# A two-layer decoder on one core: another layout of the attention rounds in both layers

## What is computed

```python
x = x + _L0_attn_ref(_layernorm(x), ...)            # gated delta-rule scan
x = x + _L0_xattn_ref(_layernorm(x), ctx, ctx, ...) # 16 heads of 16, causal
x = x + _L0_ffn_ref(_layernorm(x), ...)             # 8 experts by low-rank parts, 1024 wide
x = x + _L1_attn_ref(_layernorm(x), ...)            # state-space scan, 512 inner, projected by out_proj
x = x + _L1_xattn_ref(_layernorm(x), ctx, ctx, ...) # 16 heads of 16, not causal
x = x + _L1_ffn_ref(_layernorm(x), ...)             # product keys
```

```python
scores = jnp.einsum('bthd,bshd->bhts', Q, K) / jnp.sqrt(jnp.float32(DH))
P = jax.nn.softmax(scores, axis=-1)
out = jnp.einsum('bhts,bshd->bthd', P, V).reshape(B, Tq, D)
return out @ Wo + b_o
```

## Time and profile before

| | us |
|---|---|
| median of 3 runs | 8376.84 (8373.83 to 8382.36) |
| the profiled execution: its own time | 8381.71 |
| the profiled execution: its span | 8379.6 |
| layer 0 stage, one turn (12 turns, 1607.86 to 2242.06) | 52.85 |
| layer 1 stage, one turn (14 turns, 6071.05 to 6764.23) | 49.51 |

### The profile page before, as it was taken

One profiled execution on the slowest core, in us unless ns is written; L12 is line 12 of the kernel. 1 busy time (PEld: TensorE's weight loads), 2 busy tenths in 40 slices (PEclk: granted clock), 3 DMA queues, 4 the chain that ended last, 5 costly groups with the idle time before them and its releaser, 6 DMA issues. The chain is left out here.

```text
span 8379.6 us, 122772 instructions
## 1 busy us (share of the span) xinstructions
PE 6244.1 (75%) x40740; PEld 4178.7 (50%) x40740; DVE 6666.1 (80%) x11381; ACT 3461.7 (41%) x6666; POOL 3671.7 (44%) x1911
## 2 busy tenths in 40 slices
PE   5455554888866677777777777777677769999999
PEld 3355554677755322222222222222244448888888
DVE  6799997555567899999999999999744547676765
ACT  3333332333323566666666566666444321212121
POOL 0000000111100599999999999999611112222222
PEclk8777776999988899999999999999888879999999
DMA  2211112111022100000000000000011110000000
GB/s 63 72 42 42 42 44 61 39 36 36 19 78 108 63 14 15 15 14 15 15 14 21 19 17 14 15 15 8 29 41 36 36 66 7 8 7 8 7 8 6
DMA packets 335677, 254.47 MB, mean 30 GB/s; under 512 B 161763, under 2 KB 307046, under 8 KB 334854
## 3 DMA queue, kind: packets, MB, share of 16 engines
q1 hardware_dynamic: 332774, 248.29, 9.5%
q10 hardware_dynamic: 2464, 0.26, 0.0%
HBM read 140.46 MB, written 108.00 MB: 30 GB/s over the span
## 5 line engine op out<-in xcount | busy, mean ns | idle before, releaser
L1809 POOL TENSOR_TENSOR ss_inp<-ss_dx,ss_b_all 128x1024 f32<-128x1024 f32 x1024 | 2390.2, 2359 | 230.1 <-ACT ss_b_all L1783 227.9
L1827 DVE TENSOR_TENSOR_SCAN ss_h<-banks,ss_inp 128x1024 f32<-128x1024 f32 x1024 | 2313.0, 2278 | 59.9 <-ACT banks L1775 59.9
L1747 PE MATMUL banks<-ss_ch,ident 128*128 128x512 f32 x4096 | 1959.5, 601 | 64.9 <-DVE ss_xc L1843 64.9
L1775 ACT ACTIVATE banks<-ss_dt,ss_neg_a 128x510 f32<-128x510 f32 x2048 | 1334.7, 688 | 2.7 <-DVE ss_h L1827 2.7
L1725 PE MATMUL banks<-ss_bc,ss_pick 96*128 96x512 bf16 x2048 | 747.0, 386 | 787.8 <-DVE ss_ch L1836 750.2
L1783 ACT COPY ss_b_all<-banks 128x512 f32<-128x512 f32 x1024 | 600.4, 586 | 1235.7 <-PE banks L1725 1232.0
L1747 PEld LDWEIGHTS banks<-ss_ch,ident 128*128 128x128 f32 x4096 | 788.0, 193 | 635.9 <-issue 577.9
L1725 PEld LDWEIGHTS banks<-ss_bc,ss_pick 96*128 (+1 forms) x2048 | 200.0, 98 | 1662.7 <-issue 1484.6
L1836 DVE TENSOR_TENSOR ss_ch<-ss_h,banks 128x1024 f32<-128x1024 f32 x768 | 917.9, 1195 | 0.0
L605 PE MATMUL banks<-ms_rprod,ident 128*128 128x128 f32 x2048 | 466.8, 400 | 507.9 <-DVE ms_rprod L691 507.9
L2139 POOL TENSOR_TENSOR pk_blockhot<-pk_onehot,pk_parts 128x2048 bf16<-128x2048 bf16 x96 | 345.5, 3628 | 1099.7 <-DVE pk_parts L2377 1099.7
(11 more groups left out here) (293 smaller groups left out, 10344.9 us busy)
## 6 DMA issues: line engine op xcount, KB each, us to landing
keep_v<-ms_cx_values SPq DMA_DIRECT2D x32, 512.0 KB, 2.8
l_va<-keep_v SPq DMA_DIRECT2D x32, 512.0 KB, 5.3
l_kf<-keep_k SPq DMA_DIRECT2D x32, 256.0 KB, 4.1
keep_x<-l_x SPq DMA_DIRECT2D x32, 256.0 KB, 2.2
keep_xc<-si_xc SPq DMA_DIRECT2D x16, 512.0 KB, 3.0
keep_zs<-si_zs SPq DMA_DIRECT2D x16, 512.0 KB, 4.0
keep_dt<-si_acc SPq DMA_DIRECT2D x16, 512.0 KB, 2.6
keep_dx<-si_acc SPq DMA_DIRECT2D x16, 512.0 KB, 2.6
```

The lines of the kernel that those rows point to most:

```text
L1747: m = T_.matmul(sums[j][:, :], chip.ident[:, :], ch[u][:, j, :], start=first, stop=False, skip_group_check=True)
L1775: last = A.activation(decay[u % 2][:, j, :, 1:T], inputs[i % 2][0][:, j, :, 1:T], ACT.Exp, scale=neg_a[:, i % 2 * HB + j, bass.ds(k * UN + ...
L1809: G_.tensor_tensor(inp[u][:, :, :], inputs[i % 2][1][:, :, :, :].rearrange("p j g t -> p j (g t)"), rep(b_all[u][:, :], 1, HB), ALU.mult). ...
L1827: V.tensor_tensor_scan(flat(h[u][:, :, :]), decay[u % 2].rearrange("p j g t -> p (j g t)"), flat(inp[u][:, :, :]), 0.0, ALU.mult, ALU.add) ...
```

## The change

In both layers the scores (and their maxima) begin a round later: score s of a batch stood in round 2 + s and stands in round 3 + s of its turns, one round behind the one in which it stood; `forward_*` of layer 0 starts one round later too. `enter_vector` and `enter_scalar` are cut in two: the part up to the biased q, and `parts_*`, the split of q. Layer 0 puts them together as before, with a wait for `q_split` of the batch ahead added before the bias.

In layer 1 a turn is laid out anew. Heads start in round 7 (scores so in rounds 10 to 25), the norm and q projection of batch n + 2 in rounds 0 to 8, the split of q moves to the next turn (batch n + 1, DVE rounds 1 to 6), and the projection of the scan's output is taken out of `enter` as `mix_*`, for batch n + 3, in four quarters in rounds 19 to 22. The outer loop starts one turn earlier, and SP loads four batches ahead instead of three.

```diff
     def maxima_tensor(self, T_, b):
-        yield
-        yield
+        yield from nothing(3)
...
-    def enter_tensor(T_, b):
-        yield
+    def mix_tensor(T_, b):
         T_.wait_ge(*ys_loaded[b % 2].at(b // 2))
         if b:
             T_.wait_ge(*at.q_biased.at(b - 1))
         for t in range(NT):
-            m = project(T_, bank[at.ENTER], tiled(ys[b % 2], t), blocks(wout), col=t * C)
-            if t == NT - 1:
-                m.then_inc(ys_projected.sem, 1)
-            yield
-        yield from nothing(8)
-        yield from at.enter_tensor(T_, b)
-
-    def enter_vector(V, b):
+            for half in range(2):
+                for j in range(half * IB // 2, (half + 1) * IB // 2):
+                    m = T_.matmul(bank[at.ENTER][:, t * C:(t + 1) * C], ys[b % 2][:, j, t * P:(t + 1) * P], wout[:, j, :],
+                                  start=j == 0, stop=j == IB - 1)
+                if t == NT - 1 and half:
+                    m.then_inc(ys_projected.sem, 1)
+                yield
...
+    TURNS, MIX = 7, 19
+
     def tensor(T_):
-        for n in range(-2, B):
+        for n in range(-3, B):
             now = []
             if n >= 0:
                 now.append(at.weigh_tensor(T_, n))
             if 0 <= n + 1 < B:
-                now.append(at.maxima_tensor(T_, n + 1))
-            if n + 2 < B:
-                now.append(enter_tensor(T_, n + 2))
+                now.append(after(TURNS, at.maxima_tensor(T_, n + 1)))
+            if 0 <= n + 2 < B:
+                now.append(after(4, at.enter_tensor(T_, n + 2)))
+            if n + 3 < B:
+                now.append(after(MIX, mix_tensor(T_, n + 3)))
             if 0 <= n + 1 < B:
-                now.append(at.turns_tensor(T_, n + 1))
+                now.append(after(TURNS, at.turns_tensor(T_, n + 1)))
             rounds(now)
...
             if 0 <= n < B:
                 now.append(at.weigh_vector(V, n, x_ready))
+            if 0 <= n + 2 < B:
+                now.append(enter_vector(V, n + 2))
             if 0 <= n + 1 < B:
-                now.append(at.maxima_vector(V, n + 1))
+                now.append(after(1, at.parts_vector(V, n + 1)))
+                now.append(after(TURNS, at.maxima_vector(V, n + 1)))
             if n >= 1:
                 now.append(after(2, measure(V, n - 1)))
-            if n + 2 < B:
-                now.append(enter_vector(V, n + 2))
+            if n + 3 < B:
+                now.append(after(MIX + 4, mix_vector(V, n + 3)))
             if 0 <= n + 1 < B:
-                now.append(at.turns_vector(V, n + 1))
+                now.append(after(TURNS, at.turns_vector(V, n + 1)))
```

More of the change, by code:

```diff
@@ L896, in enter_vector, with parts_vector @@
         V.wait_ge(*self.q_projected.at(b))
+        if b:
+            V.wait_ge(*self.q_split.at(b - 1))
         V.tensor_tensor(self.qf[:, :, :], two(self.bank[self.ENTER][:, :]), rep(self.bq[:, :], 1, NT), ALU.add).then_inc(self.q_biased.sem, 1)
         yield
-        yield from nothing(2)
+    def parts_vector(self, V, b):
         V.wait_ge(*self.q_biased.at(b))
@@ L922, in enter_scalar, with parts_scalar @@
         yield
-        yield from nothing(11)
+    def parts_scalar(self, A, b):
         A.wait_ge(*self.q_split.at(b))
@@ L1270, in enter_vector, with enter_scalar @@
         yield from at.enter_vector(V, b)
+        yield from nothing(2)
+        yield from at.parts_vector(V, b)
+    def enter_scalar(A, b):
+        yield from nothing(11)
+        yield from at.enter_scalar(A, b)
+        yield from nothing(11)
+        yield from at.parts_scalar(A, b)
     def forward_tensor(T_, b):
@@ L1351, in tensor @@
             if n >= 1:
-                now.append(forward_tensor(T_, n - 1))
+                now.append(after(1, forward_tensor(T_, n - 1)))
             if 0 <= n + 1 < B:
@@ L1366, in vector @@
             if n >= 1:
-                now.append(forward_vector(V, n - 1))
+                now.append(after(1, forward_vector(V, n - 1)))
             if n + 2 < B:
@@ L1379, in scalar @@
             if n + 2 < B:
-                now.append(after(11, at.enter_scalar(A, n + 2)))
+                now.append(enter_scalar(A, n + 2))
             if 0 <= n + 1 < B:
@@ L1946, in sync @@
         load(0)
-        for n in range(-2, B):
-            if n + 3 < B:
-                load(n + 3)
+        for n in range(-3, B):
+            if n + 4 < B:
+                load(n + 4)
             if 0 <= n + 1 < B:
@@ L1964, in enter_tensor, with mix_vector @@
         for t in range(NT):
-            m = project(T_, bank[at.ENTER], tiled(ys[b % 2], t), blocks(wout), col=t * C)
-            if t == NT - 1:
-                m.then_inc(ys_projected.sem, 1)
-            yield
-        yield from nothing(8)
-        yield from at.enter_tensor(T_, b)
-    def enter_vector(V, b):
+            for half in range(2):
[5 more added lines that the diff above has]
+                yield
+    def mix_vector(V, b):
         x = at.x[b % 5]
-        yield from nothing(4)
         V.wait_ge(*at.x_loaded[b % 5].at(b // 5))
@@ L1977, in enter_vector @@
         V.tensor_tensor(x[:, :, :], x[:, :, :], two(bank[at.ENTER][:, :]), ALU.add).then_inc(mixed.sem, 1)
-        yield from nothing(3)
+        yield
+    def enter_vector(V, b):
         V.wait_ge(*mixed.at(b))
@@ L1994, in tensor @@
             if 0 <= n + 1 < B:
[L1995 to L1997 removed]
+                now.append(after(TURNS, at.maxima_tensor(T_, n + 1)))
[3 more added lines that the diff above has]
+                now.append(after(MIX, mix_tensor(T_, n + 3)))
             if 0 <= n + 1 < B:
[L1999 removed]
+                now.append(after(TURNS, at.turns_tensor(T_, n + 1)))
             rounds(now)
     def vector(V):
[L2003 removed]
+        for n in range(-3, B + 1):
             now = []
@@ L2022, in scalar @@
             if n + 2 < B:
-                now.append(after(11, at.enter_scalar(A, n + 2)))
+                now.append(after(4, at.enter_scalar(A, n + 2)))
             if 0 <= n + 1 < B:
-                now.append(at.turns_scalar(A, n + 1))
+                now.append(after(TURNS - 1, at.parts_scalar(A, n + 1)))
+                now.append(after(TURNS, at.turns_scalar(A, n + 1)))
             rounds(now)
```

1 line of the change is left out of this document (removed).

## The result

The changed kernel takes 8257.42 us (median of 4 runs, 8255.1 to 8261.42), the kernel before 8376.57 in the same comparison (4 runs, 8373.83 to 8382.36). The ratio is 0.9857, with a 95% interval of 0.9844 to 0.9869: 119 us less. The forecast was 8281 (96 us less), its range 8225 to 8345.

The account below looks back on a forecast made before the run. PE was taken to bound layer 0, no engine layer 1, whose tail is one chain. Layer 1's 70 us less and layer 0's 26 less gave -96: 8286 against the profiled execution, 8281 against the median; range 8225 to 8345.

Parts of the forecast that it names:

- Rounds 0 to 6: Layer 1's turn start, left to rescoring, then norm transpose, values and q projection: 9.7 us, bounds 8.5 and 12.
- Rounds 7 to 18: Layer 1's full rounds: twelve at 1.55 make 18.6, less waits for qT, 17.5 us; bounds 14.5 and 20.
- Rounds 19 to 26: Layer 1's tail, from ot's copy to the norm's transpose, with scores, heads and mix over it: 17.3 us, bounds 15.5 and 20.
- Contention: Layer 1's tail: POOL's k split, sharing SBUF interfaces with DVE, makes the bias add 0.55 us longer.
- The cover of POOL: Layer 1's tail: norm2's root, queued behind POOL's split, done at 14.8, under reductions until 15.6: 0.8 us to spare.
- three waits: Layer 0, PE: nmaxT behind output adds 1.0 us, round 5's kT copy 1.7, division behind feed-forward cut and q subtraction 0.9.
- The ends: Layer 1's stage: +2 us before the first turn, where first heads come later; -2 in turn 14, with less tail.
- The clock was not lost in the body: Rival, 5 in 100: PE at 1.2 GHz through layer 1's rounds 7 to 22, +10 us a turn, 8421.
- The rounds did not keep their price: Rival, 6 in 100: hand-overs rule layer 1's rounds 7 to 25 at 1.91 us each, turn 49.0, total 8344.
- Layer 0 did not lose: Rival, 12 in 100: layer 0's new waits stand and old ones stay, +1.4 us in fifteen turns, total 8328.
- A late POOL: Layer 1: POOL or va's load late by 2 us a turn, 8309; within the forecast's range, no separate chance.
- The rule on the clock: Layer 1 before the change, clock 0.86 over 49.5 us: prices 6.9 us a turn, 97 in fourteen; not taken as gain.

Follow-up runs that it names:

- the other two edits: On the changed kernel: 36 spare matmuls in layer 1's tail, layer 0's output adds behind nmaxT; 8272.97 us with heads from round 4, 8283.7 from round 3.

## Why the prediction was right

**The bound and the mechanism held.** No engine bounded layer 1; the tail's chain did, and laying scores and heads over it shortened the turn. The wo projection at 1.95, the granted clock at 0.91, the h2 transpose waiting for DVE came as forecast. In size the forecast was cautious: 119 us came where 96 were forecast, 96 and 22 by layer (by the run with layer 1 alone) where it had 70 and 26. Three terms of layer 1's sum, 44.5 us, were too large; the usual turn took 41.78:

- *Rounds 0 to 6*: 9.7 forecast, 8.83 measured. The norm was ready sooner: the transpose of h1 stands 4.54 us behind that of the maxima, not 5.2, and the clock was back in the middle of the rescoring.
- *Rounds 7 to 18*: 17.5 forecast, 16.28 measured. "Twelve make 18.6" counted twelve full rounds. The scores only begin in round 10 and the rescoring ends in round 16, so three rounds lack a pair of scores (0.22 us each) and two lack rescoring (0.43 each): 1.5 us, more than the miss. The count in the window shows it: 155 matmuls, where twelve full rounds with their three weighings of values would hold 168.
- *Rounds 19 to 26*: 17.3 forecast, 16.67 measured, with errors inside. PE reached the wo projection at 6.16 (forecast 6.45), and the last reduction ended at 14.94 (forecast 15.6). Contention was too small: the bias add took 1.41 us, 0.73 more than in a tail with POOL idle, forecast 0.55. The pair of rows behind that price had 0.70 us of a POOL instruction still ahead of the subtraction, here it was 0.87. The cover of POOL was forecast at 0.8 us and there was none. The norm starts 0.11 us behind the end of POOL's root, as in the kernel before, where it had nothing else to wait for (0.10), and with less work on POOL it came 0.13 sooner. So the root ended last by 0.13 us. The prediction had named that as a sign of being wrong. Here it cost next to nothing; with the heads three rounds later it was 6.26 us, so the thin margin at round 7 was luck and not the planned cover.

**Layer 0**: three waits were forecast at 1.0, 1.7 and 0.9 us and came at 0.96, 1.20 and 0.90, their sum with the rest at 4.1 against 4.20. The turn lost 1.44 us where the listed waits fell by 1.62. That the two are so near is luck in part: "work is unchanged, so I sum PE's waits" is the weak step, since short delays aren't listed, and with the feed-forward early the listed waits fell by 1.05 while the turn grew by 0.69. The attribution was wrong as well. I put the removed waits of scores for qT first; the run with the feed-forward early shows that the scores' distance alone costs 0.69 us, and that the delayed feed-forward on top of it brings 2.13, all of the gain and more. The fourth corner, scores early with the feed-forward late, was not run, so whether the distance helps beside the delayed feed-forward stays open.

**The ends**: +4.4 before the first turn (forecast +2), -1.0 in turn 14 (forecast -2). The load of `va`, costed at nothing, cost 1.67 us in the first turn and nothing in the others.

**The rivals.** The clock was not lost in the body (1.00 in rounds 7 to 18). The rounds did not keep their price. Layer 0 did not lose. A late POOL cost 0.13 us at round 7; at round 10 DVE waits 6.26 us a turn for it, most of what the change had won.

**The rule on the clock** (the Trainium skill, TensorE: Matmul & The Clock Gate, Terms) puts the penalty at the throttled time times (1 - K/N). Worked with the mean granted clock, that is an estimate of 42.04 x (1 - 0.91) = 3.8 us a turn for the changed kernel, and of 3.4 for a rise from 0.91 to 0.99. The measured gain is 0.66 in the usual turn and 0.64 on the mean of fourteen, (588.51 - 579.62)/14. So the trace goes against reading that figure as a gain: here the low clock costs only where PE is the one that is waited for, at the two transposes that end a turn and at the first rescorings.

## What to carry to other kernels

Count what each round of a hand-made order really holds before multiplying a round's price: rounds at either end of a pipeline lack a member. When a chain is covered with other work, the cover queues in the chain's own engines, here as reductions on DVE and as the split on POOL. Look for the second line before shortening the first: less on DVE alone brought the tail nothing, less on POOL alone 0.13 us, and a head start in round 5, which shortens both, 1.48. (Of head starts in rounds 3, 4, 5, 7 and 10 the best is 5, 3 and 4 having been run only with the other two edits. q's parts stand against an earlier one, DVE's reductions and POOL's split against a later one.) And an order can be summed from listed waits only down to the shortest wait that is listed: undo each half by itself before saying which half brought the gain.

## What the runs showed of the hardware

A DVE addition or subtraction of two 128x512 f32 operands from SBUF took 0.68 or 0.69 us with POOL idle. Where it began while an instruction of POOL's k split was in flight, it ended 0.54 or 0.55 us after that instruction did, in all 186 such places of the fourteen traces. With 0.30 us of a bf16 copy left it took 0.84 us (heads from round 5), with 0.70 left 1.24, with 0.86 left 1.41 (scores a round earlier, at 6055.32); with 0.87 us of a two-operand subtraction left it took 1.41 (the changed kernel). So the price went by how much of POOL's instruction was left, and not by which it was. POOL pays as well: an instruction of the split that began 0.48 us before the end of such an addition took 0.34 us longer, the cast 0.95 instead of 0.61 and the copy 1.38 instead of 1.04.

And 36 matmuls that compute nothing, on an engine that was not the bound, shortened a turn by 0.66 us through the granted clock.
